# Cross attention, then two layers of local attention and feed-forward: the entries into attention in another order

## The reference

```python
def reference(x, ctx_1024, L0_xattn_Wq, ..., L0_ffn_b2):
    # x (2, 2048, 512), ctx (2, 154, 512); 16 heads of 32
    def _L0_xattn_ref(query, key, value, Wq, bq, Wk, bk, Wv, bv, Wo, bo):
        ...
        scores = jnp.einsum('bhqd,bhkd->bhqk', q, k) / jnp.sqrt(jnp.float32(HD))
        attn = jax.nn.softmax(scores, axis=-1)
        out = jnp.einsum('bhqk,bhkd->bhqd', attn, v)
        ...
        return out @ Wo.T + bo

        def _layer(x, wqkv, qs, ksc, wo, lg, lb, w1, b1, w2, b2):
            # 8 heads of 64, WINDOW 256, HID 1365, 2 layers
            h = shift_token(x)              # second half of the channels from the token before
            q, k, v = jnp.split(h @ wqkv, 3, axis=-1)
            ...
            q = l2norm(q) * qs
            k = l2norm(k) * ksc
            q, k = rotary_xpos(q, k)        # q * cos * scale + rotate_half(q) * sin * scale, k likewise
            o = local_attention(q, k, v)    # each window of 256 with itself and the one before
            ...
            x = x + o @ wo
            h = shift_token(x)
            ...                             # layer norm over the channels, * lg + lb
            a, g = jnp.split(h @ w1 + b1, 2, axis=-1)
            x = x + (a * jax.nn.gelu(g, approximate=False)) @ w2 + b2
            return x
        ...
    x = x + _L0_xattn_ref(_layernorm(x, axis=-1), ctx_1024, ctx_1024, ...)
    x = x + _L0_ffn_ref(_layernorm(x, axis=-1), ...)
    return x
```

## Time and profile before

| | us |
|---|---|
| median of 3 runs | 3564.96 (3563.28 to 3565.54) |
| the profiled execution, its own time | 3564.11 |
| its span, first to last instruction | 3562.3 |
| PE busy | 3412.7 (96%) |
| DVE busy | 1955.5 (55%) |
| ACT busy | 1702.7 (48%) |
| POOL busy | 1133.0 (32%) |
| mean granted TensorE clock | 0.986 |

### The profile page before, as it was taken

How to read it: one execution, slowest core, us unless ns; L and a number is a source line. 1 busy time by engine, 2 the same in 40 slices (tenths; PEclk the granted TensorE clock), 3 DMA queues, 4 the chain that set the end, 5 groups by cost and what they waited for, 6 DMA issues and landing times. The chain is left out here.

```text
span 3562.3 us, 56374 instructions
## 1 busy us (share of the span) xinstructions
PE 3412.7 (96%) x20560; PEld 2797.1 (79%) x20560; DVE 1955.5 (55%) x4484; ACT 1702.7 (48%) x4490; POOL 1133.0 (32%) x1008
## 2 busy tenths in 40 slices
PE   7999996999999989999999979999999899999999
PEld 5666675888888877888888858888888778888887
DVE  6888875677777764223323247776777643233322
ACT  5666663677777763111111137777777521111111
POOL 3434433555555520000000035555555121101111
PEclk9999998999999999999999989999999999999999
DMA  4112213111221122111111111112111331111111
GB/s 123 42 46 65 72 42 125 37 60 60 65 67 61 61 87 83 44 44 43 43 44 44 64 65 51 61 61 65 64 60 58 120 100 49 36 46 50 45 37 38
DMA packets 186869, 216.26 MB, mean 61 GB/s; under 512 B 27094, under 2 KB 125654, under 8 KB 186595
## 3 DMA queue, kind: packets, MB, share of 16 engines
q1 hardware_dynamic: 186595, 212.65, 18.6%
HBM read 125.79 MB, written 69.00 MB: 55 GB/s over the span
## 5 line engine op out<-in xcount | busy, mean ns | idle before, releaser
L1917 DVE SCALAR_TENSOR_TENSOR u_full<-banks,b_cols,gate 128x512 f32<-128x512 f32 (+1 forms) x176 | 132.1, 750 | 877.2 <-ACT gate L1875 803.8
L1875 ACT ACTIVATE gate<-banks,b_cols 128x512 f32<-128x512 f32 (+1 forms) x176 | 121.3, 689 | 1008.3 <-PE banks L48 1008.3
L46 PE MATMUL banks<-fxT_h,w_h 128*128 128x512 f32 (+1 forms) x1408 | 556.7, 395 | 2.6 <-DVE w_l L1901 2.4
L48 PE MATMUL banks<-fxT_h,w_l 128*128 128x512 f32 (+1 forms) x1408 | 556.9, 395 | 0.0
L47 PE MATMUL banks<-fxT_l,w_h 128*128 128x512 f32 (+1 forms) x1408 | 555.9, 395 | 0.0
L1770 POOL TENSOR_TENSOR sums<-sums,b_rows 128x512 f32<-128x512 f32 x64 | 85.5, 1368 | 878.7 <-DMA sums<-z_rows 878.7
L46 PE MATMUL banks<-wqkv_h,hT_h 128*128 128x512 f32 x768 | 325.7, 424 | 15.8 <-DVE wqkv_l L1435 14.4
L46 PEld LDWEIGHTS banks<-fxT_h,w_h 128*128 128x128 f32 (+1 forms) x1408 | 260.2, 185 | 70.3 <-DVE w_l L1901 3.7
L48 PEld LDWEIGHTS banks<-fxT_h,w_l 128*128 128x128 f32 (+1 forms) x1408 | 260.8, 185 | 67.4
L47 PEld LDWEIGHTS banks<-fxT_l,w_h 128*128 128x128 f32 (+1 forms) x1408 | 260.5, 185 | 67.1
L48 PE MATMUL banks<-wqkv_h,hT_l 128*128 128x512 f32 x768 | 305.0, 397 | 0.0
(11 more groups left out here) (190 smaller groups left out, 8095.3 us busy)
## 6 DMA issues: line engine op xcount, KB each, us to landing
y_rows<-sums SPq DMA_DIRECT2D x16, 1024.0 KB
sums<-y_rows SPq DMA_DIRECT2D x64, 256.0 KB, 2.9
z_rows<-sums SPq DMA_DIRECT2D x64, 256.0 KB, 2.0
sums<-z_rows SPq DMA_DIRECT2D x16, 1024.0 KB, 5.6
thirds<-in_w SPq DMA_DIRECT2D x30, 512.0 KB, 4.9
thirds<-in_x SPq DMA_DIRECT2D x8, 1024.0 KB, 6.9
x_rows<-thirds SPq DMA_DIRECT2D x8, 1024.0 KB, 4.3
thirds<-y_rows SPq DMA_DIRECT2D x64, 128.0 KB, 2.8
```

Source lines behind the costliest of these rows:

```text
L46: pe.matmul(out, a_h, b_h, start=start, stop=False)
L48: return pe.matmul(out, a_l, b_h, start=False, stop=stop)
L1875: e.activation(gate[r, :], ps[r, 2 * (m % 2) + 1, :], ACT.Gelu, bias=b1[r, place[m], 1:2]).then_inc(s["ac_g"], 1)
L1917: e.scalar_tensor_tensor(out=u_full[r, m % 2, :], in0=ps[r, 2 * (m % 2), :], scalar=b1[r, place[m], 0:1], in1=gate[r, :], op0=ALU.add, op1 ...
```

## The change

It has parts in four places.

Cross attention's last group: the moments' epsilon, the root and the normalisation go tile by tile (4 small instructions each on VectorE and GpSimd instead of 1), VectorE normalises tile t behind the moments of tile t+1, the x1 store becomes four DMAs of 256 KB, and behind each tile's store and normalisation SP loads one of the weight pieces 4 to 7.

Attention's SP list: the v pieces (8 to 11) stand first, then the scales, then the first rotary table, then the mask, then wo. GpSimd waits for the small tables only ahead of scaling a table. In tile 0 the scaling comes behind the root of q.

GpSimd, in all tiles: the root of k stands ahead of sin and sum of q instead of behind them.

The prologue of attention: TensorE waits for weights per piece instead of per four; it projects q and k of tile 1 ahead of the transposes of the rotated tile 0, which get PSUM banks of their own (`bank_r`); the wait of q of tile 1 is for the normalised k of tile 0; k of tile 1 waits for nothing but h. ScalarE squares k ahead of rounding the v pieces, and rounds wo behind v and h of tile 1. VectorE makes wo's low parts behind v, k and h of tile 1, and normalises q of tile 1 behind the low parts of the rotated tile 0.

```diff
@@ -553,10 +554,21 @@
                 e.wait_ge(st_x1, 16 * (NG - 1))
-                for n in range(ahead["pieces"]):
+                for n in range(GT):
                     load_piece(e, ahead["s"], ahead["w"], n)
-                store_before(Group(NG, NG, 0), NG)
-                e.wait_ge(st_x1, 16 * NG)
+                def load_last(tt):
+                    e.wait_ge(st_last[tt], 16)
+                    e.wait_ge(dv_y, GT * (NG - 1) + tt + 1)
+                    load_piece(e, ahead["s"], ahead["w"], GT + tt)
+                for tt in range(GT):
+                    e.wait_ge(dv_x1, GT * (NG - 1) + tt + 1)
+                    e.dma_start(rows(dram["x1"], (NG - 1) * G)[:, tt], x_in[:, (NG - 1) % XSLOTS, tt]).then_inc(st_last[tt], 16)
+                    if tt:
+                        load_last(tt - 1)
+                load_last(GT - 1)
+                store_y(Group(NG, NG, 0), NG)
             @block.gpsimd
@@ -599,7 +611,9 @@
                 run(e, body)
-                root_y(NG - 1)
+                for tt in range(GT):
+                    e.wait_ge(dv_vy, NG + tt)
+                    e.tensor_tensor(rs_y[:, tt:tt + 1], ve_y[:, tt:tt + 1], neg_half[:, 0:1], ALU.pow).then_inc(pl_ry, 1)
             @block.tensor
@@ -878,14 +892,19 @@
                     mark(e.bn_aggr(mv_y[:, tt, :], stats_y[:, tt, :]))
-                    if tt == GT - 1:
+                    if it == NG - 1:
+                        settle()
+                        e.tensor_scalar(ve_y[:, tt:tt + 1], mv_y[:, tt, 1:2], EPS, None, ALU.add).then_inc(dv_vy, 1)
+                    elif tt == GT - 1:
                         settle()
...
                 def finish(it, slot, tt):
+                    if it == NG - 1:
+                        e.wait_ge(pl_ry, NG + tt)
+                    elif tt == 0:
+                        e.wait_ge(pl_ry, it + 1)
                     if tt == 0:
-                        e.wait_ge(pl_ry, it + 1)
                         e.wait_ge(st_y, 32 * it + (16 if it * G >= N else 0))
@@ -943,8 +962,9 @@
                     moments_y(NG - 1, slot, tt)
-                for tt in range(GT):
-                    finish(NG - 1, slot, tt)
+                    if tt:
+                        finish(NG - 1, slot, tt - 1)
+                finish(NG - 1, slot, GT - 1)
 def attention_sems(sem):
@@ -1050,7 +1070,7 @@
         def bank_r(t, a):
-            return turn(7 * t + 2 + a)
+            return turn(7 * t + 2 + a) if t else S_BANK + 1 + a
         def bank_head(h):
@@ -1114,7 +1134,8 @@
                         store(i, u - 1)
-                load_weights(dram["pieces"], w.slots)
+                load_weights(w.slots, 3 * DC)
                 for a, name in enumerate(("q_scale", "k_scale")):
@@ -1122,9 +1143,9 @@
                                     src[:, (1 - half) * DH // 2:(2 - half) * DH // 2].to_broadcast([P, DH // 2])).then_inc(s["ld_small"], 16)
+                load_tables(0, 0)
                 e.dma_start(mask[:], io["mask"]).then_inc(s["ld_small"], 16)
-                load_tables(0, 0)
-                load_weights(w.slots, w.count)
+                load_weights(3 * DC, w.count)
                 load_tables(0, 1)
@@ -1136,26 +1157,27 @@
             def _(e):
-                e.wait_ge(s["ld_small"], 16 * SMALL * (l + 1))
                 def rotate(i, j):
...
                     base = l * NI + (i + j // 4) + 1
-                    e.wait_ge(s["ld_rot"][u], 16 * base)
-                    e.tensor_tensor(rot[:, u], rot[:, u], qk_scale[:], ALU.mult).then_inc(s["pl_tab"], 1)
-                    e.wait_ge(s["pl_tab"], at(NT, i, 4, j + 1))
                     hd = DH // 2
...
                     tabs = [rot[:, u, a, :].rearrange("p (o d) -> p o d", o=1) for a in range(4)]
+                    def scale_table():
+                        e.wait_ge(s["ld_rot"][u], 16 * base)
+                        e.wait_ge(s["ld_small"], 16 * SMALL * (l + 1))
+                        e.tensor_tensor(rot[:, u], rot[:, u], qk_scale[:], ALU.mult).then_inc(s["pl_tab"], 1)
                     def root(a):
...
                     def times_cos(a):
+                        e.wait_ge(s["pl_tab"], at(NT, i, 4, j + 1))
                         e.wait_ge(s["dv_norm"], at(2 * NT, i, 8, 2 * j + a + 1))
@@ -1171,10 +1193,16 @@
                         e.tensor_tensor(y1, y1, y2, ALU.add).then_inc(s["pl_rot"], 1)
-                    for a in range(2):
-                        root(a)
-                        times_cos(a)
-                        plus_sin(a)
+                    if (i, j) != (0, 0):
+                        scale_table()
+                    root(0)
+                    if (i, j) == (0, 0):
+                        scale_table()
+                    times_cos(0)
+                    root(1)
+                    plus_sin(0)
+                    times_cos(1)
+                    plus_sin(1)
                 rotate(0, 0)
@@ -1204,11 +1232,15 @@
                     e.wait_ge(s["dv_h"], nth(NT, t + 1))
-                    if a == 1:
+                    if (t, a) == (1, 0):
+                        e.wait_ge(s["dv_norm"], nth(2 * NT, 2))
+                    elif a == 1 and t > 1:
                         e.wait_ge(s["dv_r"], nth(2 * NT, 2 * t - 1))
...
                     for k in range(DC):
+                        if t == 0:
+                            e.wait_ge(w_lo, w.done(DC * a + k + 1))
                         last = split_matmul(e, ps[:, bank_qkv(t, a), :], [x[:, k, :] for x in hT],
@@ -1219,7 +1251,9 @@
                         e.wait_ge(s["pl_rot"], nth(2 * NT, 2 * t + a + 1))
-                        if a == 0:
+                        if t == 0:
+                            pass
+                        elif a == 0:
                             e.wait_ge(s["dv_y"], nth(NT, t - 2))
@@ -1287,12 +1321,11 @@
                 for a in range(3):
-                    e.wait_ge(w_lo, w.done(DC * (a + 1)))
                     project(0, a)
                 transpose_h(1)
-                transpose_qk(0)
                 project(1, 0)
                 project(1, 1)
+                transpose_qk(0)
                 scores(0, 0)
@@ -1392,14 +1425,14 @@
                 squares(0, 0)
+                squares(0, 1)
                 round_weights(2 * DC, 3 * DC)
-                squares(0, 1)
-                round_weights(3 * DC, w.count)
                 hi_v(0)
                 hi_h(1)
-                hi_qk(0)
+                round_weights(3 * DC, w.count)
                 squares(1, 0)
                 squares(1, 1)
+                hi_qk(0)
                 for h in range(LANES):
@@ -1515,15 +1548,15 @@
                 norms(0, 1)
+                lo_v(0)
+                normalise(0, 1)
+                lo_h(1)
                 rest_of_weights(3 * DC, w.count)
-                normalise(0, 1)
+                norms(1, 0)
+                norms(1, 1)
+                lo_qk(0)
+                normalise(1, 0)
                 e.wait_ge(s["ld_small"], 16 * SMALL * (l + 1))
-                lo_v(0)
-                lo_h(1)
-                lo_qk(0)
-                norms(1, 0)
-                normalise(1, 0)
-                norms(1, 1)
                 for h in range(LANES):
```

More of the change, by code:

```diff
@@ L127, in build @@
     x_st_y = sem("x_st_y")
-    X_PIECES = SLOTS["w_attn"] // 2
     def cross_is_stored(e):
@@ L162, in build @@
                     dict(ctx_k=ctx_k, ctx_v=ctx_v, x1=x1_rows, y=y_rows, late=y_late, st_y=x_st_y), keep, sums,
-                    dict(s=attn_s, w=attn_w[0], h_in=h_in, dram=y_from_cross, pieces=X_PIECES))
+                    dict(s=attn_s, w=attn_w[0], h_in=h_in, dram=y_from_cross))
     for l in range(DEPTH):
@@ L169, in build @@
         attention_phase(nc, io, ps, ident, attn_s, neg_half, l, h_in, sums, attn_w[l],
-                        dict(y_from_ffn if l else y_from_cross, dst=z_rows, dst_late=z_late, pieces=SLOTS["w_attn"] if l else X_PIECES),
+                        dict(y_from_ffn if l else y_from_cross, dst=z_rows, dst_late=z_late),
                         dict(s=ffn_s, w=ffn_w[l], t=ffn_in, dram=dict(src=z_rows, src_late=z_late)))
@@ L173, in build @@
                   dict(src=z_rows, src_late=z_late, is_stored=attention_is_stored, dst=y_rows, dst_late=y_late, x1=x1_rows),
-                  dict(s=attn_s, w=attn_w[l + 1], h_in=h_in, dram=y_from_ffn, pieces=SLOTS["w_attn"]) if l + 1 < DEPTH else None)
+                  dict(s=attn_s, w=attn_w[l + 1], h_in=h_in, dram=y_from_ffn) if l + 1 < DEPTH else None)
     ctx.close()
@@ L437, in cross_phase @@
     st_x1, st_y, pl_xb = sem("x_st_x1"), dram["st_y"], sem("x_pl_xb")
+    st_last = [sem(f"x_st_last{tt}") for tt in range(GT)]
     pe_s, dv_max, ac_exp, dv_rc, pl_p = sem("x_pe_s"), sem("x_dv_max"), sem("x_ac_exp"), sem("x_dv_rc"), sem("x_pl_p")
@@ L515, in store_before @@
                 def store_before(g, it):
-                    r, r_late = g.row(e, -1), g.row(e, -1, 1)
                     e.wait_ge(dv_x1, GT * it)
```

(7 more changed lines are left out.)

## The result

The changed kernel takes 3540.38 us, median of 4 runs (3538.53 to 3541.7), against 3564.12 (3561.26 to 3565.54) on the same chip: ratio 0.9934, interval 0.9917 to 0.9951. The forecast was 3548.3 us, with a range from 3542 to 3556. The sign was right and the size was not: 23.7 us were gained for 16.7 forecast, and the time lies 1.6 us under the range. A second set gave 3540.99 us against 3564.07, ratio 0.9932 (0.9919 to 0.9944).

A forecast was written before the change was run, and what follows sets the result against it. TensorE was taken as the bound, almost always busy in full tiles but idle at attention's entries. Layer 0 10.0, layer 1 5.9 and hand-over 0.8 make 16.7 us: 3564.1 to 3547.4, plus 0.85 for the median, 3548.3; range 3542 to 3556.

The forecast's parts named there:

- The first tiles: Entry into attention: tile 2's q projection starts 10.0 us earlier in layer 0 and 5.9 in layer 1.
- u: The prediction's time in us, counted from the first transposition of h in a layer's attention entry.
- The waits named: TensorE at the entries: 1.9 us before v, 3.7 before tile 1's q; tile 0's 6.5 and 8.6 rotation waits gone.
- The recorded sum: GpSimd's steps for tile 1's rotation, after its normalised q at 31.7: sum 9.75 us, to 41.6.
- The hand-over: From cross attention to attention: finishing the last group tile by tile gains 0.8 us.
- Small tables: Loaded after v: GpSimd's table product done at 15.4, wanted at 15.7; hidden by 0.3 us, otherwise 0 to 3 a layer.
- a sign of error: Listed under "Wrong": GpSimd's first table product in attention's entry released by a DMA.
- rival A: Tables late at the entries: GpSimd's first product waits and what follows moves; 3553.3 us, chance 0.10.
- B: Rival: TensorE's clock stays low over both projections of tile 1 after the idles; 3553.1 us, chance 0.10.
- C: Rival: TensorE has high clock for tile 1's projections; 3543.5 us, chance 0.06.
- The root ahead of sin and sum, in all tiles: GpSimd in full tiles: k's root moved forward has 1.2 us of cover before TensorE comes; value taken: nothing.
- The bounds of the sum: Tile 1's clock 2.4 us a layer either way, tables 0 to 3 a layer, hand-over 0 to 1.4; ends 5.1 and 22.1.

The follow-up runs named there:

- after: The changed kernel itself, as against the kernel before the change: 3540.38 us against 3564.12.
- a_root2on: The changed kernel with the old order of the roots on GpSimd in tiles 0 and 1 alone, early root from tile 2 on: 3543.96 us.
- a_tables: The changed kernel with scales, mask and first rotation table loaded ahead of the v pieces again: 3541.42 us.
- a_best: The changed kernel with tile 0's root of k ahead of the table product, k's squares summed earlier on VectorE, two wo low parts later: 3534.25 us.
- a_root01: The changed kernel with the early root of k in tiles 0 and 1 alone, old GpSimd order from tile 2 on: 3545.05 us.
- b_root: The kernel before with one edit: GpSimd takes the root of k ahead of q's sin and sum in every tile: 3550.69 us.
- a_nocross: The changed kernel without the new end of cross attention (last group finished whole, four weight pieces loaded there): 3541.13 us.
- after_again: The changed kernel, unchanged, run and profiled a second time: 3540.99 us.

## Why the prediction was wrong in size

**The first tiles: right.** The forecast went step by step in u. In the two profiles of after, both layers, tile 0's v projection starts at 12.1 to 13.7 (forecast 13.0), tile 1's q projection at 20.3 to 20.7 (20.1), and tile 2's q projection at 41.4 to 42.6 (42.1). The waits named were there: 2.0 between k and v, 2.7 to 3.6 for 3.7, no long wait of tile 0's transposes, tile 1's rotated k the last to wait. Layer 0 gave 9.5 and 10.5 us for 10.0, layer 1 6.3 and 6.6 for 5.9. What I did not see is how much of it hangs on the root in tiles 0 and 1 (a_root2on: 2.8 to 4.0 us an entry).

The recorded sum has a slip of 0.15 us: 31.7 and 9.75 make 41.45, not 41.6.

**The hand-over: right in kind, small in size,** 1.2 us for 0.8. Behind the last output projection VectorE was done normalising 1.6 us sooner (forecast 1.4), and SP's added load took 0.4 of it back (forecast 0.5). Of the 3.1 us that the pair of profiles shows, 1.9 lie ahead of that projection's end.

**Small tables: hidden but for a few tenths.** I had named a first product released by a DMA as a sign of error, and so it was released:

```profile
591.25 0.74 POOL L1173 TENSOR_TENSOR rot<-rot,qk_scale 128x256 f32<-128x256 f32 x1 [3.57 <-DMA mask<-in_mask]
```

It ended at u = 16.2 for 15.4, and the normalised q was there at 16.0 for 15.7; a_tables, whose tables come early, is no faster. So rival A did not come. B and C did not either: tile 1's q projection ran at a clock of 0.50 to 0.65 and took 4.2 to 5.3 us, and k behind it took 2.9 to 3.0 us, which is the full clock. In a_best, with a shorter wait ahead of q, C's condition did come.

**The step that failed** is "The root ahead of sin and sum, in all tiles", value taken "nothing". It measured 2.5 to 2.6 us a layer, 5.1 in all (a_root01, with b_root from the other side). 16.7 + 5.1 = 21.8 from the forecast's own terms; with the hand-over and the entries as measured the sum is 1.2 + 9.5 to 10.5 + 6.3 to 6.6 + 5.1 = 22.1 to 23.4. The medians gave 23.7 and 23.1, with intervals of 6 and 4 us to either side, so what is left can't be told from chance.

It failed in three ways. I asked only when GpSimd ends and TensorE comes for its result, at 713.98, and found 1.2 us of cover. I did not ask who else waits for the root: VectorE does, at the head of its queue, and what it has behind is wanted earlier. I did not follow the root into the next tile either, over the residual's sums and SP's store to the load of the table. And I took the price from one full tile for tiles that are not full. The stage's idle time was in my own rows, 657.04 - 651.71 = 5.3 us. I used it as a ceiling for the gain and did not look where it lay: 3.1 of it in the two steps above. The bounds of the sum did not take it in either, and so the lower end of the range, 3542 us, lay too high.

## What to carry to other kernels

When an instruction is moved forward on one engine, follow not only the engine that takes the final result but each engine whose queue stands still at an intermediate one, and price what is behind it there. Do it for the queue that issues the DMAs too: a load can stand behind a store that waits for the moved chain. Stages with a steady step have other steps at their seams (here the first tiles of a sequence, with fewer keys): look where in the stage the bound engine's few idle microseconds are before calling them unreachable. When two profiles differ by a microsecond or two at a seam, compare the granted clock there first, and measure the edit between two fixed instructions right around it.

## What the runs showed of the hardware

The clock of TensorE at identical instructions differs between executions: 1.00 and 0.81 over 557 to 566, with 2 us (a_nocross, b_root) and 0.4 us (after, after_again) at the start of the next phase, and 1.00 and 0.97 over the 60 us at attention's end, worth 1.5. Parts of the changed kernel that look like gains in one pair of profiles (1.9 of the 3.1 us at the hand-over, 1.6 at attention's end) are of this size.

GpSimd's root of 128x8 elements takes 1.65 us, more than its product over 128x512 (1.28 to 1.30). The root over 128x4 at cross attention's end took 1.01 us, and the last one over 128x1 in after 0.78.
